# Recurrent core of a two-layer decoder: the first form of the triangular inverse, written by GpSimd instead of by identity products on TensorE

## The reference

```
def step(Sst, inp):
    q_t, k_t, v_t, a_t, b_t = inp
    Sst = Sst * a_t[..., None, None]
    kv = jnp.einsum('bhd,bhde->bhe', k_t, Sst)
    delta = (v_t - kv) * b_t[..., None]
    Sst = Sst + jnp.einsum('bhd,bhe->bhde', k_t, delta)
    o_t = jnp.einsum('bhd,bhde->bhe', q_t, Sst) * scale
    return (Sst, o_t)
```

## Time and profile before

| | us |
|---|---|
| median of 3 runs | 7478.29 (7475.86 to 7489.34) |
| the profiled execution, its own time | 7497.67 |
| its span, first to last instruction | 7494.8 |
| the recurrent core in the span | about 2975 to 3985 |
| mean granted TensorE clock over the span | 0.887 |

### The profile page before, as it was taken

The page is one execution under the profiler, slowest core; times in us unless marked ns, Lnnn a source line. Parts: engine busy times, 40 slices in busy tenths (PEclk is TensorE's granted clock), DMA queues, the critical chain, the costliest instruction groups (busy, mean ns, idle before and its releaser), DMA issues. The chain is left out here.

```text
span 7494.8 us, 148096 instructions
## 1 busy us (share of the span) xinstructions
PE 5680.7 (76%) x53564; PEld 3328.7 (44%) x53580; DVE 4389.8 (59%) x8417; ACT 3054.7 (41%) x4533; POOL 2156.5 (29%) x1704
## 2 busy tenths in 40 slices
PE   5488888888833597888897888442558888889998
PEld 2255555556712243777775555321212222244444
DVE  4599999997766554444443443545457777523333
ACT  2399999994422253222222332000015555511111
POOL 0288778885500133444442111111000000000000
PEclk7699999999966798999999999666659999989999
DMA  2302020101100134223322011122232222110000
GB/s 79 80 21 44 14 48 18 35 14 52 49 17 20 65 146 153 96 99 102 104 99 69 34 42 34 28 41 67 76 72 35 35 37 35 41 41 22 17 17 16
DMA packets 417078, 395.75 MB, mean 53 GB/s; under 512 B 232106, under 2 KB 371231, under 8 KB 408343
## 3 DMA queue, kind: packets, MB, share of 16 engines
q1 hardware_dynamic: 402711, 363.20, 17.4%
q10 hardware_dynamic: 13824, 25.17, 0.9%
HBM read 248.02 MB, written 140.23 MB: 52 GB/s over the span
## 5 line engine op out<-in xcount | busy, mean ns | idle before, releaser
L441 POOL TENSOR_SCALAR attn_u<-attn_rel,attn_aux 128x1024 f32<-128x1024 f32 x512 | 1090.4, 2130 | 274.9 <-DVE attn_nm L468 273.5
L2887 DVE TENSOR_REDUCE attn_mx<-attn_mp 128x1 f32<-128x512 f32 x1024 | 641.3, 683 | 218.5 <-PE attn_mp L2976 199.7
L592 PE MATMUL attn_tp<-attn_ident,attn_pr 128*128 128x128 f32 x4096 | 573.1, 284 | 243.3 <-ACT attn_pt L531 241.0
L460 DVE SCALAR_TENSOR_TENSOR attn_u<-attn_rel,attn_aux,attn_u 128x1024 f32<-128x1024 f32 x512 | 679.8, 1328 | 30.3 <-POOL attn_u L441 18.3
L2958 ACT ACTIVATE attn_pt<-attn_st 128x1024 f32<-128x1024 f32 x512 | 509.2, 1022 | 432.9 <-PE attn_st L2986 432.4
L592 PEld LDWEIGHTS attn_tp<-attn_ident,attn_pr 128*128 128x128 f32 x4096 | 449.5, 143 | 465.2 <-ACT attn_pt L531 326.6
L468 DVE CUSTOM_DVE_ANT_0 attn_pr<-attn_u,attn_s 128x1024 f32<-128x1024 f32 x512 | 619.5, 1210 | 47.5 <-PE attn_s L583 37.7
L552 ACT ACTIVATE attn_pr<-attn_pr,attn_nm 128x1024 f32<-128x1024 f32 x512 | 603.1, 1178 | 85.2 <-DVE attn_nm L468 85.0
L531 ACT ACTIVATE attn_pt<-attn_tp 128x512 f32<-128x512 f32 x1024 | 566.1, 622 | 14.1 <-issue 7.7
L2976 PE MATMUL attn_mp<-attn_kt,attn_qt 96*128 96x512 bf16 x1024 | 376.8, 403 | 114.6 <-DVE attn_mx L2887 68.0
L3356 PE MATMUL moe_ps<-moe_w,moe_hidt 128*128 128x512 f32 x1024 | 453.2, 594 | 0.0
(11 more groups left out here) (481 smaller groups left out, 10709.3 us busy)
## 6 DMA issues: line engine op xcount, KB each, us to landing
s_qkv<-gin_qkv SPq DMA_DIRECT2D x32, 1536.0 KB, 5.1
core_qk<-s_qkv SPq DMA_DIRECT2D x32, 1024.0 KB, 5.0
attn_qt<-s_q SPq DMA_DIRECT2D x384, 64.0 KB, 3.0
attn_kt<-s_k SPq DMA_DIRECT2D x192, 128.0 KB, 4.4
core_arow<-s_alr SPq DMA_DIRECT2D x32, 512.0 KB, 3.8
core_grow<-s_gar SPq DMA_DIRECT2D x32, 512.0 KB, 3.7
core_vv<-s_qkv SPq DMA_DIRECT2D x32, 512.0 KB, 3.6
s_o<-core_o ACTq DMA_DIRECT2D x32, 512.0 KB, 3.7
```

Source lines behind the costliest of these rows:

```text
L441: pool.tensor_scalar(u[:, x % 4], rel[:, z % 2, 1], aux[:, s, 4 + NH + h:5 + NH + h], aux[:, s, 4 + 2 * NH + h:5 + 2 * NH + h], ALU.mult, ...
L460: dve.scalar_tensor_tensor(u[:, x % 4], rel[:, z % 2, 0], aux[:, slot_of(k, z), 4 + h:5 + h], u[:, x % 4], ALU.mult, ALU.add).then_inc(m[" ...
L592: ins = pe.transpose(tp[k][:, n], pr[:, x % BUF, (4 * k + n) * P:(4 * k + n + 1) * P], ident[:])
L2887: dve.reduce_max(mx[w % 2][:].rearrange("p h t a -> p (h t a)")[:, j:j + 1], mp[j % 2][:], AX.X).then_inc(m["max_done"], 1)
```

## The change

GpSimd, at the end of the step in which it finished `bt` of chunk `a`, writes `um` of that chunk: four multiplications, one for each block row of 32 partitions, of the diagonal blocks of `bt` with the mask `first` (the transposed level-0 mask, loaded in place of the identity `i32`), with a semaphore `u0_done`. `product(0)` and `masked(0)` are gone. `turned(0)` of the next step transposes `um` to `tm`, where it went from `tm` to `um`, and still signals `um_done`; `product(1)` waits for it, and has taken over the waits that `product(0)` had. The other levels keep their work, with their semaphore counts shifted.

```diff
-        i32 = r.sb("i32", [P, W32])
-        lvl = r.sb("lvl", [P, LV, W32])
+        lvl, first = r.sb("lvl", [P, LV, W32]), r.sb("first", [P, W32])
 ...
                 if a is not None:
                     unit_diagonal(1)
+                    y = x + 2
+                    pause(pool, "bt_done", a * NG + NG)
+                    if q is not None:
+                        pause(pool, "lx_mm", q * 7 + 6)
+                    for j in range(NJ):
+                        ins = pool.tensor_tensor(um[blk(j)], bt[blk(j), y % 2, :, blk(j)],
+                                                 first[blk(j)].rearrange("p (o n) -> p o n", o=1).to_broadcast([W32, GH, W32]), ALU.mult)
+                    ins.then_inc(m["u0_done"], 1)
+                    pause(pool, "u0_done", a + 1)
 ...
                 def turned(l):
                     if l == 0:
-                        need(dve, "xm_done", q * LV + 1)
+                        need(dve, "u0_done", q + 1)
+                        need(dve, "t64_done", q)
+                        dve.transpose(flat(tm[:]), flat(um[:])).then_inc(m["um_done"], 1)
                     else:
                         need(dve, "tm_c", q * 4 + l)
-                    dve.transpose(flat(um[:]), flat(tm[:])).then_inc(m["um_done"], 1)
+                        dve.transpose(flat(um[:]), flat(tm[:])).then_inc(m["um_done"], 1)
 ...
                     residual(0)
                     residual(1)
                 if q is not None:
-                    masked(0)
                     turned(0)
 ...
-                    if l == 0:
+                    if l == 1:
                         pause(pe, "bt_done", q * NG + NG)
                         pause(pe, "u6_done", q)
-                    elif l == 1:
-                        pause(pe, "xm_done", q * LV + 1)
+                        pause(pe, "um_done", q * LV + 1)
                     else:
                         pause(pe, "tm_c", q * 4 + l - 1)
                     for h in range(GH):
                         for j in range(NJ):
                             ins = pe.matmul(lx[blk(j), h * W32:(h + 1) * W32], bt[blk(j), y % 2, h, blk(j)],
-                                            tm[blk(j), h] if l else i32[blk(j)], start=True, stop=True)
+                                            tm[blk(j), h], start=True, stop=True)
 ...
                     from_state(0)
                     from_state(1)
-                if q is not None:
-                    product(0)
                 if a is not None:
                     turn(0)
                     turn(1)
 ...
-    out["eye32"] = fold(eye)
+    out["level0t32"] = fold((eye - below(1)).T).astype(np.float32)
```

More of the change, by code:

```diff
@@ L1441, in stage_gdn_core @@
         names = ("w_in prep consts alr_mm alr_c gar_done alr_zero rows_out ar_in ib_done db_done kp_done tr_done kq_c ktq_done gk_done at_done "
-                 "bt_done lx_mm lt_mm xm_done um_done tm_c x5_c t10_c x6_c u5_done u6_done ufd_done t64_done "
+                 "bt_done lx_mm lt_mm xm_done um_done tm_c x5_c t10_c x6_c u0_done u5_done u6_done ufd_done t64_done "
                  "ks_done r_done w_done dl_done qs_done o_mm o_c ds_done sd_done s_done "
@@ L1476, in _ @@
         def _(sp):
-            for dst, src in ((ident[:], d["ident"]), (i32[:], d["eye32"]), (lvl[:], d["levels32"]),
+            for dst, src in ((ident[:], d["ident"]), (first[:], d["level0t32"]), (lvl[:], d["levels32"]),
                              (alog[:], d["L1_attn_A_log"].partition_broadcast(P)), (dtb[:], d["L1_attn_dt_bias"].partition_broadcast(P)),
@@ L1665, in _ @@
                     inverse(4)
-                    need(act, "lx_mm", q * 8 + 6)
+                    need(act, "lx_mm", q * 7 + 5)
                     for j in (1, 3):
@@ L1731, in masked @@
                 def masked(l):
-                    need(dve, "lx_mm", q * 8 + l + 1)
-                    dve.tensor_tensor((xm if l else tm)[:], heads(lx[:, 0:GH * W32], W32),
+                    need(dve, "lx_mm", q * 7 + l)
+                    dve.tensor_tensor(xm[:], heads(lx[:, 0:GH * W32], W32),
                                       lvl[:, l].rearrange("p (o n) -> p o n", o=1).to_broadcast([P, GH, W32]), ALU.mult
@@ L1796, in _ @@
                     y = x + 1
-                    need(dve, "lx_mm", q * 8 + 7)
+                    need(dve, "lx_mm", q * 7 + 6)
                     dve.tensor_copy(uf[blk(0), y % 2, :, blk(1)], heads(lx[blk(0), 0:GH * W32], W32))
@@ L1803, in _ @@
                 if q is not None:
-                    need(dve, "lx_mm", q * 8 + 8)
+                    need(dve, "lx_mm", q * 7 + 7)
                     dve.tensor_copy(uf[0:64, y % 2, :, 64:], heads(lx[0:64], 64)).then_inc(m["u6_done"], 1)
@@ L1856, in product @@
                             ins = pe.matmul(lx[blk(j), h * W32:(h + 1) * W32], bt[blk(j), y % 2, h, blk(j)],
-                                            tm[blk(j), h] if l else i32[blk(j)], start=True, stop=True)
+                                            tm[blk(j), h], start=True, stop=True)
                     ins.then_inc(m["lx_mm"], 1)
                 def update(l):
-                    pause(pe, "xm_done", q * LV + l + 1)
+                    pause(pe, "xm_done", q * 4 + l)
                     for h in range(GH):
```

## The result

The changed kernel takes 7510.36 us (median of 8 runs, 7499.54 to 7522.51), the kernel before 7481.99 (median of 8, 7473.16 to 7489.34). The ratio is 1.0038, with a 95% interval of 1.0029 to 1.0048: 28 us slower, between 22 and 36. 7482 had been forecast, with 7458 to 7503 as the range.

A forecast was written before the change was run, and what follows sets the result against it. TensorE was taken to bound the recurrent core, close to the pace of its instruction supply. The terms -22 (`product(0)`), +46 (the new wait) and -20 (instruction supply) gave +4 us, 7482, range 7458 to 7503.

The forecast's parts named there:

- Part 1 and 2: Each chunk: dropping `product(0)` saves 0.68 us of TensorE, 22 us in all; dropping `masked(0)`, 0.42 us of VectorE, gives nothing.
- Part 3: GpSimd's four multiplications before `product(1)`: it starts 0.74 us later a chunk, +24 us with the removals included.
- Part 4: VectorE and GpSimd work queued behind the chain: `update(1)` still covers `masked(1)`, `kp` comes some 0.6 later, no added cost.
- Part 5: TensorE's instruction supply: 4096 fewer instructions, 16 of 207 packets, shorten its stalls; 20 us taken, range 0 to 35.
- the first rival: `product(1)` waits as forecast but TensorE's instruction stalls stay as long: +24 us, 7502, range 7495 to 7525; chance 0.26.

The follow-up runs named there:

- the wide fill: The changed kernel with three wide idle matmuls for each chunk behind `from_state`, in TensorE's wait: ratio 1.0036, +27 us against the kernel before.
- a third piece, with the moved residual: GpSimd's multiplications in three pieces (heads 0-3, 4-5, 6-7), `turned(0)` between VectorE's two residuals: ratio 1.0005, +4 us against the kernel before.
- the narrow fill: The changed kernel with the 32 identity products of `product(0)` written twice for each chunk in TensorE's wait: ratio 1.0099, +74 us against the kernel before.

## Why the prediction was wrong

- **Part 1 and 2, what goes.** Right for the typical chunk.
- **Part 3, the new chain: +24 us predicted, and 24 by the mean over the chunks.** The mechanism and the place hold: 0.73 us for a multiplication was forecast by the earlier trace rows, 0.718 is the mean. That the sum agrees as well as it does is in part luck, for two things that were not foreseen cancel: in the typical chunk `product(1)` is 0.92 us later where 0.74 was forecast, and where a turn of the loop begins it is not later at all. What was short in the typical chunk is the small things: GpSimd's wait for its own `bt` 0.34 for 0.27, the four together 3.05 for 2.92, and 0.14 for 0.1 between VectorE and TensorE.
- **Part 4, what queues behind.** Right: `update(1)` comes at 3434.91 without a wait, `kp` is not waited for.
- **Part 5, the refund of 20 us: this is the step that failed.** It said that 16 packets fewer would shorten the stalls, 8 us in proportion and 17 because the packets left hold more work. The packets did go (207 to 186 in the stretch). The `issue` waits of the 32x32 groups, 74 us before, had been forecast at 55. They are 60 and 68 us in the two profiles of the changed kernel, but 74 again (54.9 + 19.2) in that with 128 instructions ahead, and the time shows nothing of a refund: the later start alone gives 24 of the 28 us. With nearly equal time on TensorE the fewer instructions gave nothing (+3 us with an uncertainty of about 9), and with `product(0)` put back the kernel was not 20 us slower but 13 to 19 faster. The faulty step is the 0.25 us by which every packet that is left was to last longer. That is an average over all packets; a packet in the crowded groups later in the step holds the same instructions as before and lasts as long, and only those around the old place of `product(0)` have changed. The prediction had itself noted that this stretch is the one without stalls, and took only 5 us off for it; it should have taken nearly all. By the first rival, the wait without the refund, the loss would have been 24 us; that is the case that came, at 26% in the prediction. It was put at 7502, from a median before of 7478; from the 7482 of the eight runs it is 7506, against 7510 measured.
- **The range** ended at 7503, which takes in 8 of the 30 us of this rival (7495 to 7525) and not most of it, as was said. With a quarter of the chance on it, a range for 8 in 10 should have reached well into it.
- **The clock** was left out. After the wait of 1.7 us the next products ran partly at the lower clock (`solve(0)` 1.77 us for 1.16), and the stage's granted clock fell by 0.02. What it cost is open: the kernel with `product(0)` kept had a better clock and was 13 to 19 us faster than the changed one, the wide fill had the same better clock and was not. Both have the same start of `product(1)`, and their stalls differ by 14 us (68 and 82). Why they do is not shown; other places of the packet boundaries are the candidate.

On the Trainium skill's rule ("Runtime: NRT & Kernel Launch", section "Instruction fetch mechanics": the fetch of 16 KiB blocks is hidden): this case's traces contradict it, with stalls a packet apart and 45 us for 29 more packets in the narrow fill; its answer for this change, no term, was nevertheless nearer to what was measured than the 20 us.

## What to carry to other kernels

Work moved to an idle engine is free only while nobody waits for its end. What counts is the distance from the last input to the first reader: here 3.4 us of GpSimd and 0.6 us with the transpose, at a place where TensorE had 2.3 us of other work left (from the end of `bt` at 3428.52 to 3430.84). If it must stand there, cut it so that only the part that depends on the last input stands behind it; in two halves the kernel was 14 us faster than before, and a third piece, with the moved residual, brought no earlier start, because of the waits between the pieces, and lost the gain.
A stall that is spread over a stage is not refunded by removing instructions where it does not occur. Ask which stall stands behind the removed instructions, and price that one.

## What the runs showed of the hardware

TensorE's stalls on its instruction supply stand at the same instruction in each turn of the loop, a packet or a multiple of it apart. Eight chunks behind the stalls at 3404.67 and 3409.91 the same groups are cut at the same place, 23 and 37 records before their end:

```profile
3659.90 0.39 PE L1865 MATMUL core_lt<-core_xm,core_um 32*32 32x32 f32 x23 [1.61 <-issue]
...
3665.14 0.52 PE L1865 MATMUL core_lt<-core_xm,core_um 32*32 32x32 f32 x37 [1.66 <-issue]
```

With 128 instructions ahead of the loop (64 matmul records and 64 loads) the stalls of the first chunk of the first turn came 63 matmul records earlier, after 219, 344 and 470 of them from the start of `from_state`, where it was 282, 407 and 533. Shifting the loop in this way cost 12 us (interval 4 to 20) by 64 instructions, and by 128 3 us (-4 to 9). A difference of 10 us between two kernels with such loops is not yet evidence on their work.
A GpSimd multiplication of two dense inputs over 32 partitions took 0.312 us for 64 elements, 0.449 for 128 and 0.718 for 256: by these three an estimate of a fixed 0.18 us and 2.1 ns an element. Over 128 partitions 256 elements took 0.728, so fewer partitions gained next to nothing.
Where the loop goes back for its second and its third turn, TensorE stood still for 3.5 to 4.1 us ahead of `from_state` in both kernels (4.05 and 3.60 before, 3.52 and 3.93 changed).
